# Score quads of an attention and expert kernel on one core: four PSUM banks handed over as one instead of in two pairs

## What is computed

```python
x = x + 0.5 * ffn(layernorm(x))      # job rows 0..7 of the kernel
x = x + dilated_attention(layernorm(x))
x = x + 0.5 * ffn(layernorm(x))      # job rows 8..15, the same weights
# ffn: 16 heads of 8 features, causal
scores = einsum('bhqd,bhkd->bhqk', q, k) / sqrt(8)
attn = softmax(where(causal, scores, min))
h = layernorm(x + (attn @ v) @ w_o, g1, b1)
# then the two best of 8 experts (128 -> 512 -> 128, gelu), weighted, and a layernorm
```

## Time and profile before

| what | value |
|---|---|
| runs | 1195.87, 1197.24, 1200.68 us, median 1197.24 |
| the profiled execution | span 1192.8 us, 29724 instructions; the profile gives no other time of its own |
| busy PE, DVE, ACT, POOL | 1022.4, 680.8, 670.5, 572.7 us |
| granted TensorE clock, mean over the span | 0.90 of 2.4 GHz |
| exponentials L706 | 256 of 128x768, 193.7 us busy |
| selects L1173 | 256 of 128x512, 182.5 us busy |
| maxima L874, L875 | 256 and 256, 149.9 and 80.5 us busy |

### The profile page before, as it was taken

The page is one execution under the profiler, slowest core; times in us unless marked ns, Lnnn a source line. Parts: engine busy times, 40 slices in busy tenths (PEclk is TensorE's granted clock), DMA queues, the critical chain, the costliest instruction groups (busy, mean ns, idle before and its releaser), DMA issues. The chain is left out here.

```text
span 1192.8 us, 29724 instructions
## 1 busy us (share of the span) xinstructions
PE 1022.4 (86%) x10913; PEld 818.6 (69%) x10913; DVE 680.8 (57%) x2458; ACT 670.5 (56%) x1494; POOL 572.7 (48%) x693
## 2 busy tenths in 40 slices
PE   4799979998989989999989989998999988866470
PEld 2566656886877867686777867687777866766470
DVE  5657665655558835686568835686556723520314
ACT  1243424875758756675667757576666756534240
POOL 2223356235465455555565455554464456542515
PEclk9988877998999989898999979799999979887795
DMA  3394105555555545555556545555556545676562
GB/s 71 86 193 109 37 19 162 167 164 181 154 160 150 172 138 156 147 154 172 149 154 171 165 137 144 153 158 154 160 163 176 170 137 164 202 244 221 212 194 51
DMA packets 117239, 181.01 MB, mean 152 GB/s; under 512 B 13128, under 2 KB 80232, under 8 KB 117096
## 3 DMA queue, kind: packets, MB, share of 16 engines
q1 hardware_dynamic: 108904, 162.32, 47.7%
q0 software_dynamic: 8192, 16.79, 4.9%
HBM read 145.10 MB, written 38.68 MB: 154 GB/s over the span
## 5 line engine op out<-in xcount | busy, mean ns | idle before, releaser
L1173 POOL TENSOR_SCALAR_AFFINE_SELECT probs<-probs 128x512 f32<-128x512 f32 x256 | 182.5, 721 | 262.1 <-ACT probs L706 257.1
L706 ACT ACTIVATE probs<-ps_quad 128x768 f32<-128x768 f32 x256 | 193.7, 807 | 150.3 <-PE ps_quad L527 87.8
L744 ACT ACTIVATE act<-ps_ring,weights 128x128 f32<-128x128 f32 x696 | 191.8, 387 | 96.4 <-PE ps_ring L623 48.0
L874 DVE TENSOR_REDUCE shift_cols<-ps_quad 128x2 f32<-128x512 f32 (+3 forms) x256 | 149.9, 586 | 139.8 <-PE ps_quad L508 125.6
L632 PE MATMUL ps_ring<-weights,act 128*128 128x128 f32 x1392 | 190.8, 285 | 31.1 <-issue 16.4
L632 PEld LDWEIGHTS ps_ring<-weights,act 128*128 128x128 f32 x1392 | 174.5, 198 | 35.1 <-issue 21.6
L623 PE MATMUL ps_ring<-tile_t,weights 128*128 128x128 f32 x1392 | 187.6, 292 | 3.9 <-issue 3.2
L623 PEld LDWEIGHTS ps_ring<-tile_t,weights 128*128 128x128 f32 x1392 | 174.0, 204 | 16.8 <-issue 13.2
L1236 POOL DMA_INDIRECT picked<-sorted_outputs,place x128 | 123.7, 966 | 79.8 <-issue 78.6
L999 DVE TENSOR_TENSOR tile_y<-ps_ring,weights 128x128 f32<-128x128 f32 x174 | 48.8, 287 | 182.2 <-PE ps_ring L632 101.2
L1222 POOL DMA_INDIRECT sorted_rows<-h_rows,place x128 | 124.5, 972 | 53.5 <-issue 34.6
(11 more groups left out here) (165 smaller groups left out, 1531.5 us busy)
## 6 DMA issues: line engine op xcount, KB each, us to landing
weights<-expert_weights SPq DMA_DIRECT2D x174, 578.0 KB
tile_rows<-sorted_rows SPq DMA_DIRECT2D x56, 192.0 KB
sorted_outputs<-tile_y SPq DMA_DIRECT2D x56, 192.0 KB
query_key_parts<-qk SPq DMA_DIRECT2D x32, 256.0 KB, 5.0
k<-query_key_parts SPq DMA_DIRECT2D x64, 64.0 KB
q<-query_key_parts SPq DMA_DIRECT2D x64, 64.0 KB
sorted_rows<-zeros SPq DMA_DIRECT2D x2, 1472.0 KB, 10.7
xs<-in_L_attn_x SPq DMA_DIRECT2D x32, 64.0 KB, 2.3
```

The costliest lines, as they stand in the source:

```text
L706: sc.activation(probs[:, r % PROBS, 2 * a:2 * a + 2, :], ps_quad[:, 2 * a:2 * a + 2, 0:3 * P], ACT.Exp, scale=HD ** -0.5).then_inc(pair_fr ...
L744: ins = sc.activation(act[:, k % ACTS, f, :], bank(use)[:, f * P:(f + 1) * P], ACT.Gelu_apprx_tanh, bias=weights_of(k)[:, 2 * F + f:2 * F ...
L874: dve.tensor_reduce(shift_cols[:, late, groups], ps_quad[:, groups, 0:split], AX.X, ALU.max)
L1173: pool.affine_select(out=both, in_=both, compare_op=ALU.is_ge, fill=0.0, base=0, pattern=[[0, 2], [0, 2], [1, P]], channel_multiplier=-1). ...
```

## The change

The pair semaphores become one `quad_full` and one `quad_free`. On TensorE the four strips' matmuls of one line are issued one behind another, then those of the next line. The readers take all four banks with one instruction: one exponential of 128x1536, one select of 128x1024, one maximum for the late blocks and one for the early ones. All that waited on the second pair waits on the quad.

```diff
-        pair_full, pair_free = sems("pair_full", 2), sems("pair_free", 2)
+        quad_full, quad_free = sem("quad_full"), sem("quad_free")
...
-                for a in range(2):
-                    if no:
-                        pe.wait_ge(pair_free[a], no)
-                    for j in (2 * a, 2 * a + 1):
...
+                if no:
+                    pe.wait_ge(quad_free, no)
+                for j in range(GROUPS):
+                    rows = slice(32 * j, 32 * j + SLOT)
+                    pe.matmul(ps_quad[:, j, 0:split],
...
+                for j in range(GROUPS):
+                    rows = slice(32 * j, 32 * j + SLOT)
+                    pe.matmul(ps_quad[:, j, split:9 * SLOT],
...
+                mm.then_inc(quad_full, 1)
...
-                for a in range(2):
-                    pe.wait_ge(pair_free[a], QUAD_NO["exps", n, j])
-                    for i in (2 * a, 2 * a + 1):
...
+                pe.wait_ge(quad_free, QUAD_NO["exps", n, j])
+                for i in range(4):
+                    rows = slice(32 * i, 32 * i + SLOT)
+                    pe.matmul(ps_quad[:, i, 0:P], k4[rows, par, j, at + P:at + S], q4s[rows, n % 2, j, P:S],
+                              start=True, stop=True, tile_position=(32 * i, 0))
+                for i in range(4):
+                    rows = slice(32 * i, 32 * i + SLOT)
+                    mm = pe.matmul(ps_quad[:, i, P:3 * P], k4[rows, par, j, at:at + P], q4s[rows, n % 2, j, :],
+                                   start=True, stop=True, tile_position=(32 * i, 0))
+                mm.then_inc(quad_full, 1)
...
-                pe.wait_ge(selected, 2 * EXP_NO["exps", n, j] + 2)
+                pe.wait_ge(selected, EXP_NO["exps", n, j] + 1)
...
-                for a in range(2):
-                    pair_used(sc, ("exps", n, j), a)
-                    sc.activation(probs[:, r % PROBS, 2 * a:2 * a + 2, :], ps_quad[:, 2 * a:2 * a + 2, 0:3 * P], ACT.Exp,
-                                  scale=HD ** -0.5).then_inc(pair_free[a], 1)
+                quad_used(sc, ("exps", n, j))
+                sc.activation(probs[:, r % PROBS, :, :], ps_quad[:, :, 0:3 * P], ACT.Exp,
+                              scale=HD ** -0.5).then_inc(quad_free, 1)
...
-                for a in range(2):
-                    groups = slice(2 * a, 2 * a + 2)
-                    pair_used(dve, ("scores", n, i), a)
-                    dve.tensor_reduce(shift_cols[:, late, groups], ps_quad[:, groups, 0:split], AX.X, ALU.max)
-                    dve.tensor_reduce(shift_cols[:, soon, groups], ps_quad[:, groups, split:9 * SLOT], AX.X, ALU.max
-                                      ).then_inc(pair_free[a], 1)
+                quad_used(dve, ("scores", n, i))
+                dve.tensor_reduce(shift_cols[:, late, 0:GROUPS], ps_quad[:, :, 0:split], AX.X, ALU.max)
+                dve.tensor_reduce(shift_cols[:, soon, 0:GROUPS], ps_quad[:, :, split:9 * SLOT], AX.X, ALU.max
+                                  ).then_inc(quad_free, 1)
...
-                for a in range(2):
-                    pair_emptied(pool, ("exps", n, j), a)
-                    both = probs[:, r % PROBS, 2 * a:2 * a + 2, 0:2 * P].rearrange("p i (b q) -> p i b q", b=2)
-                    pool.affine_select(out=both, in_=both, compare_op=ALU.is_ge, fill=0.0, base=0,
-                                       pattern=[[0, 2], [0, 2], [1, P]], channel_multiplier=-1).then_inc(selected, 1)
+                quad_emptied(pool, ("exps", n, j))
+                every = probs[:, r % PROBS, :, 0:2 * P].rearrange("p i (b q) -> p i b q", b=2)
+                pool.affine_select(out=every, in_=every, compare_op=ALU.is_ge, fill=0.0, base=0,
+                                   pattern=[[0, 4], [0, 2], [1, P]], channel_multiplier=-1).then_inc(selected, 1)
```

More of the change, by code:

```diff
@@ L283, in freed, with quad_used, quad_emptied @@
             eng.wait_ge(free_sem(piece), RING_NO[piece] // RING + 1)
[L285 to L289, removed]
+        def quad_used(eng, piece):
+            eng.wait_ge(quad_full, QUAD_NO[piece] + 1)
+        def quad_emptied(eng, piece):
+            eng.wait_ge(quad_free, QUAD_NO[piece] + 1)
         NORM, MID, END, LONG = range(4)
@@ L382, in spread @@
                 elif m >= 2:
-                    pair_used(sp, ("exps", 2 * m - 3, GROUPS - 1), 1)
+                    quad_used(sp, ("exps", 2 * m - 3, GROUPS - 1))
                 elif m == 0 and which:
@@ new lines, in scores @@
+                for j in range(GROUPS):
+                    rows = slice(32 * j, 32 * j + SLOT)
+                    pe.matmul(ps_quad[:, j, 0:split],
+                              q_heads[rows, n % 2, late, :, :].rearrange("p h q -> p (h q)"),
+                              qk[rows, m % 2, 1, at:at + split],
+                              start=True, stop=True, tile_position=(32 * j, 0))
+                for j in range(GROUPS):
+                    rows = slice(32 * j, 32 * j + SLOT)
+                    pe.matmul(ps_quad[:, j, split:9 * SLOT],
+                              q_heads[rows, n % 2, soon, :, :].rearrange("p h q -> p (h q)"),
+                              qk[rows, m % 2, 1, at:at + SLOT * (soon + 1)],
+                              start=False, stop=True, tile_position=(32 * j, 0), skip_group_check=True)
@@ new lines, in scores @@
+                for j in range(GROUPS):
+                    rows = slice(32 * j, 32 * j + SLOT)
+                    diagonal = ps_quad[:, j, SLOT * late:9 * SLOT].rearrange("p (b k) -> p b k", k=SLOT)
+                    mm = pe.matmul(diagonal[:, ::soon + 1, :],
+                                   four_ident[rows, :, :].rearrange("p h q -> p (h q)"),
+                                   block_mask[rows, :].unsqueeze(1).broadcast_to([SLOT, 2, SLOT]),
+                                   start=False, stop=True, tile_position=(32 * j, 0), skip_group_check=True)
@@ L693, in project @@
                         sc.wait_ge(parts_out[which], 16 * (m - 1))
[L694 removed]
+                        quad_used(sc, ("scores", 2 * m - 3, GROUPS - 1))
                     full(sc, ("project", m, which))
@@ L860, in expand @@
                 if n >= 2:
-                    pair_used(dve, ("scores", n - 2, GROUPS - 1), 1)
+                    quad_used(dve, ("scores", n - 2, GROUPS - 1))
                 for h in range(4):
@@ L870, in scores @@
                 split = SLOT * (late + 1)
-                for a in range(2):
-                    groups = slice(2 * a, 2 * a + 2)
-                    pair_used(dve, ("scores", n, i), a)
-                    dve.tensor_reduce(shift_cols[:, late, groups], ps_quad[:, groups, 0:split], AX.X, ALU.max)
-                    dve.tensor_reduce(shift_cols[:, soon, groups], ps_quad[:, groups, split:9 * SLOT], AX.X, ALU.max
-                                      ).then_inc(pair_free[a], 1)
+                quad_used(dve, ("scores", n, i))
+                dve.tensor_reduce(shift_cols[:, late, 0:GROUPS], ps_quad[:, :, 0:split], AX.X, ALU.max)
+                dve.tensor_reduce(shift_cols[:, soon, 0:GROUPS], ps_quad[:, :, split:9 * SLOT], AX.X, ALU.max
+                                  ).then_inc(quad_free, 1)
             def shift(n):
                 par = n // 2 % 2
-                for a in range(2):
-                    pair_emptied(dve, ("scores", n, GROUPS - 1), a)
+                quad_emptied(dve, ("scores", n, GROUPS - 1))
                 step(dve.transpose(shift_rows[:, :], shift_cols[:, :, :].rearrange("p b r -> p (b r)")))
@@ L884, in shift @@
                 if n >= 2:
-                    pair_used(dve, ("exps", n - 2, GROUPS - 1), 1)
+                    quad_used(dve, ("exps", n - 2, GROUPS - 1))
                 settle()
```

1 line of the change is left out of this document (removed).

## The result

The changed kernel takes 1219.34 us (median of 4), the kernel before 1198.44: a ratio of 1.0173, with a 95% interval of 1.014 to 1.0207. It is slower by 21 us. The forecast was no change, 1200 us in a range of 1183 to 1215; rival A, slower, was right in its sign and too small in its size (1210).

What follows compares the result with a forecast made beforehand. TensorE's in-order stream, busy 86% of the span, was taken as the bound. Terms +0.7 on TensorE, -1 for less work elsewhere and +3 for the clock gave +3 us: 1200 us from 1197.24, range 1183 to 1215.

Steps and rivals of the forecast that it cites:

- rival A: Slower, 1210 us, chance 0.35: lost overlap from split exponential quad to next score quad, with five half-clock stretches.
- 0.06 us saved per exponential: On ScalarE, one exponential of 128x1536 replaces two of 128x768, saving 0.06 us; ends 0 and 0.19.
- The stand of 0.6 us at the turn: After a split exponential quad, TensorE finishes two transposes, then stands 0.6 us before the next score quad.
- Lost: the overlap: ScalarE no longer starts on a split exponential quad's first pair, so the next score quad waits: +11.1 us on TensorE.
- eleven dear turns: Score quads behind exponential quads split by over 0.56 us with little work behind: eleven places, +6.9 us.
- nineteen weaker ones: The same turns, but with exponential quads less split or more slack between: nineteen places, +4.2 us.
- earlier releases: Quads held back by their second pair start earlier: 65 exponential quads gain 5.2 us, 45 score quads 2.7 us.
- the order: On TensorE the four strips' first passes start closer: 0.01 us per quad, 256 times, -2.5 us; ends 0 and -7.
- the clock: TensorE idles more visibly, above all in the ramp: two more half-clock stretches, +3 us; ends 0 and +15.
- less work elsewhere: VectorE has 17 us and ScalarE 8 us less work, so their other pieces finish sooner: -1 us.
- Its point of decision: The slower case was to decide from about four extra half-clock stretches of TensorE on.
- The first pair's head start buys TensorE nothing: A split quad on TensorE ends where the later release puts it, however early its first pair starts.

Runs made afterwards that it cites:

- e4: The change, but TensorE issues strips 0 and 1 through all lines, then 2 and 3, behind one wait: 1.0201 of the kernel before.
- e9: The change itself once more, on another chip: 1220.88 us, ratio 1.0183 to the kernel before.
- e15: The change itself once more, as reference on the chip of three further kernels: 1.0173 of the kernel before.
- e18: The change plus extra TensorE matmuls of constants ahead of each score quad of sequences n < 10: 1.0126 of the kernel before.
- e8: The kernel before plus extra TensorE matmuls of constants ahead of each score quad of sequences n < 10: ratio 1.0098 to it without them.
- e1: Against the kernel before, only score quads change hands as one; exponential quads stay in pairs: ratio 1.0177.
- e3: Against the kernel before, only TensorE waits for both pairs and issues four strips in a row; all readers stay in pairs: ratio 1.0375.
- e2: Against the kernel before, only exponential quads change hands as one; score quads stay in pairs: ratio 1.0257.
- the moved kernel before: The kernel before with the third score quad of every sequence placed later: 1.0121 on the 1053 us chip, 1.0062 on another.
- e17: The kernel before with the third score quad of every sequence placed later, run beside the change: 1.0062 of the kernel before.
- e14: The kernel before with the third score quad of every sequence placed later, on the 1053 us chip: 1.0121 of the kernel before.
- the moved change: The change with the third score quad of every sequence placed later: 1.0207 of the kernel before on the 1053 us chip, 1.016 on another.

## Why the prediction was wrong, step by step

- **The local prices held.** 0.06 us saved per exponential: two took 1.49 to 1.52 us, one takes 1.45. The stand of 0.6 us at the turn of the earlier trace rows is 0.61 us. The strips already ran together, and their order was worth nothing that can be measured (e4). The Trainium skill (TensorE: Matmul & The Clock Gate, Part 3) says that matmuls start strictly in program order; in the earlier trace rows all eight passes of L523 start ahead of L527 (307.98 against 308.31), though half of them stand behind it in the program.
- **The step that failed is the term "Lost: the overlap" in the sum on TensorE.** It was put at 11.1 us: 6.9 for eleven dear turns and 4.2 for nineteen weaker ones. I compared the traces piece by piece, each piece from the end of the one before it on TensorE to its own end, three traces of the change (the first one, e9, e15) against the one of the kernel before. In them 32, 31 and 32 score quads lose over 0.5 us each, together 26.3, 26.9 and 25.5 us. All 128 score quads lose 21.4, 23.4 and 21.5 us net, where the sum had 7.1 (11.1 less 2.7 for earlier releases and 1.3 for the order). The price of a dear turn was near, 0.63 us against some 0.8 on average. Their number was three times too small. Many of those left out are in the ramp, where 11 to 14 score quads before the landmark lose over 0.5 us: there, as in the turn shown above, a score quad follows its exponential quad with nothing in between, and it loses even where that exponential quad was hardly split.
- **The small gains were not the mistake.** The exponential quads gain 6.7, 4.1 and 6.7 us net, where the sum had 6.5 (5.2 for earlier releases and 1.3 for the order).
- **The rest of TensorE's work** loses another 9.2, 9.3 and 8.8 us, where the forecast had 2 (+3 for the clock, -1 for less work elsewhere). What part of this is the clock is open. Of the 11.6 us at the landmark only 3.7 stand in pieces that ran at full clock in both traces, so in the ramp most of the loss lies where at least one of the two ran at the lower clock. But a loss of this size comes without a lower clock too (e4), and raising the clock did not give it back (e18, e8).
- **Rival A named the mechanism** (the overlap lost at the turn from a split exponential quad, with the clock) and the right side, at 0.35. Its point of decision, about four half-clock stretches more (some 14 us), is met in two traces of the change: 181 us at the lower clock from 60 to 1000 us, against 160 before. But e9 with 167, e4 with 167 and e1 with 156 lose as much, so this does not decide.
- **"The first pair's head start buys TensorE nothing"** misled me. It buys ScalarE an early start, and e3, which takes that head start away and has only the strip order besides, costs 1.0375, more than double of the whole change.

## What to carry to other kernels

Here, where producer and consumer alternate on one buffer, handing it over in halves was worth more than the fixed cost of the second instruction: the first half lets the next engine start while this one waits, and this passes from engine to engine. All links had to be in halves; one that waited for the whole buffer cost as much as all of them (e1, e2). In a sum over many places of an in-order engine, a right price is not enough: count the dear places over the whole run, the ramp included, where little other work stands between two turns and hides nothing.

## What was not expected of the hardware

The same kernel before took 1188 to 1201 us on the other chips and 1053 us on one. Of one and the same program, the moved kernel before, there is a trace on either kind of chip: 1216.1 us (e17) and 1064.5 us (e14). A part of the difference lies in stretches in which TensorE stood inside one group of matmuls, with no wait that the profile can name: before L632 and L540 this comes to 26.1 and 12.1 us in e17, and to nothing in e14. One such group in the kernel before, and the same group in e14:

```profile
286.29 1.17 PE L540 MATMUL ps_ring<-probs,values 128*32 128x256 f32 x4 [1.02 <-issue]
287.72 2.04 PE L540 MATMUL ps_ring<-probs,values 128*32 128x256 f32 x4 [0.26 <-issue]
289.88 0.37 PE L544 MATMUL ps_ring<-probs,values 128*32 128x128 f32 x1
290.58 0.70 PE L544 MATMUL ps_ring<-probs,values 128*32 128x128 f32 x7 [0.33 <-issue]
```

```profile
280.99 0.64 PE L540 MATMUL ps_ring<-probs,values 128*32 128x256 f32 x8
281.44 0.40 PE L544 MATMUL ps_ring<-probs,values 128*32 128x128 f32 x8
```

Sixteen passes take 5.0 us on one chip and 0.85 on the other; the granted clock is 0.51 in that stretch of the kernel before. What holds them up was not tried, and where the larger part of the difference between the chips comes from is open. On both kinds of chip the moved change loses against the kernel before by a like share, 1.016 and 1.0207.
